# Layer 1's attention: products with the values in blocks of 32 tokens

## The chip, the cores and the metric

One core of one Trainium2 chip runs one program of four transformer-like layers. The metric is the device time of one execution in microseconds. All engines of the core take part: TensorE (PE in the rows, its weight loads PEld), VectorE (DVE), ScalarE (ACT), GpSimd (POOL), and SyncE (SP), which issues most DMAs.

## What is computed

The change touches only the attention of layer 1, a dilated attention without projections. Of 64 tokens of a segment, each head sees the 32 that have its parity, and within these it is a plain softmax attention with queries, keys and values all equal to the input:

```
w, r, H, hd = 64, 2, 16, 16            # segment, dilation, heads, head size
g = gather(xs, tokens 2*k + h % 2 of the segment)          # 32 tokens for each head
scores = einsum("bnhqd,bnhkd->bnhqk", g, g) * hd ** -0.5
out = einsum("bnhqk,bnhkd->bnhqd", softmax(scores), g)     # scattered back to the same tokens
x = x + out + moe(x_normalised)
```

The other half of layer 1 is a mixture of 32 experts, 4 per token. There are 4 x 512 = 2048 tokens of 256 channels. The normalised rows are sorted by expert: for each of a token's 4 choices its row is written to a slot in DRAM by an indirect DMA.

## The kernel before

The stage `slots_route` (line 2597) of layer 1 holds everything here. Tokens lie in 16 tiles of 128; tile n = 2g + p holds the tokens of parity p of a group g of 256, so a tile is four segments' worth of 32 tokens that attend to each other, and only the 8 heads of parity p have anything to do in it. The stage normalises x, computes the router's logits, picks 4 experts for each token and works out, on VectorE, the slot of each of the 4 x 16 x 128 rows. GpSimd then issues 64 scatters (`scatter`, line 2484, the instruction at L2487), each of one tile's 128 rows to one choice of expert; it begins as soon as the first choice's slots are known. VectorE goes on with the table of blocks and the weights of the experts (L2813 to L2841). Only then, in the program order of VectorE, comes `then.vector(dve)`, the attention.

`Attention1` (line 814) works tile by tile, with two buffers for everything (index p):

- ScalarE: `key_rows` copies the normalised rows, transposed, with the other parity's heads set to zero (L899); `weights` takes the exponential of the scores (L910); `copy_sums` copies the products with the values out of PSUM (L916); `value_rows` fills the values, 16 columns a head beside a column of ones, padded to 32 (L904).
- TensorE: `scores` multiplies 8 heads' keys by themselves, each a strip of 32 rows (16 of them zero) and 128 x 128 tokens (L859). `values` multiplies, for each of 8 heads, the values (128 tokens by 32 columns) by the exponentials (128 by 128 tokens), giving sums that are channel by token (L868). `back` turns them to token by channel, two transposes a tile (L876).
- VectorE: `mask` multiplies the exponentials (128 x 1024) by a 0/1 matrix that keeps the blocks of 32 tokens on the diagonal (L943). `finish` takes the reciprocal of the sums of the ones' column (L950), scales (L952) and adds to x (L957).
- The order is written out by hand in each engine's loop, by one tile ahead; semaphores count tiles. `mask`, `finish` alternate on VectorE; `scores`, `values`, `back` on TensorE.
- GpSimd: `wait_under_way` lets lot n of 8 scatters start only when 2(n - 2) + 1 masks are done, so that the attention's steps aren't held up behind them.

float32 matmuls show in the trace as two passes, each with a weight load, so 8 matmuls are 16 instructions.

The stage ends with a barrier of all engines. The next one, `slots_experts` (f_ in the names), loads the slots and begins its products. SyncE issues the loads of the biases (L2546, L2548) after VectorE has released its scratch, right ahead of the attention.

## Time and profile before

| | us |
|---|---|
| median of 3 runs (lowest, highest) | 2124.78 (2124.61, 2125.85) |
| the profiled execution | 2104.8 |
| its span, first to last instruction | 2102.9 |
| TensorE, VectorE, ScalarE, GpSimd busy | 1800.2, 1394.7, 740.2, 578.4 |
| mean granted TensorE clock | 0.925 |

The span is cut into stages by barriers. The one of this change lies at 130 to 261 us of the span, its attention at 170 to 226, its scatters at 164 to 256. An instruction's row in the timeline gives its start, its duration, and, in brackets, how long its engine was idle before it and who released it; "PEq L2651" and "POOLq L2651" are the barrier between two stages.

### The profile page before, as it was taken

The numbers are of one execution on the slowest core, as the hardware profiler recorded it, in microseconds if no ns is written. First come the engines' busy times: TensorE is split into PE (matmuls) and PEld (weight loads), VectorE is DVE, ScalarE is ACT, GpSimd is POOL, SyncE is SP. The second block draws the span as 40 slices with busy tenths as digits, with TensorE's granted clock in tenths as the row PEclk, the third lists the DMA queues.
The fourth block names the chain that finished last, engine by engine and source line by source line (L and its number), as shares of the span: only waits on it lengthen the run. The fifth ranks groups of instructions, "written<-read, shape, count | busy, mean of one in ns | idle before, by whom it ended". The sixth has DMA issues, their size and how long they took to land. (4 is left out here: it accounts for less than half of the span.)

```text
span 2102.9 us, 37015 instructions
## 1 busy us (share of the span) xinstructions
PE 1800.2 (86%) x13832; PEld 1433.3 (68%) x13832; DVE 1394.7 (66%) x2980; ACT 740.2 (35%) x1733; POOL 578.4 (28%) x550
## 2 busy tenths in 40 slices
PE   5844189944999999999999997999988997989995
PEld 2432177833899999999899985455566875767773
DVE  5588255548787777777787775666656777644444
ACT  2424134422333343434333333145534323322221
POOL 1326735540121221212221112622232103511111
PEclk9976699975999999999999997989998996999998
DMA  9448244443000000000000100000001007111114
GB/s 324 142 132 269 88 136 146 149 150 111 1 1 24 24 2 24 1 24 1 24 1 24 34 1 1 0 1 2 2 1 53 29 1 251 62 43 48 49 49 140
DMA packets 103060, 134.86 MB, mean 64 GB/s; under 512 B 11628, under 2 KB 78984, under 8 KB 102376
## 3 DMA queue, kind: packets, MB, share of 16 engines
q1 hardware_dynamic: 91800, 102.01, 15.5%
q0 software_dynamic: 11088, 30.49, 4.0%
q8 instruction: 116, 1.90, 0.4%
q14 instruction: 56, 0.46, 0.1%
HBM read 81.92 MB, written 50.54 MB: 63 GB/s over the span
## 5 line engine op out<-in xcount | busy, mean ns | idle before, releaser
L1138 POOL TENSOR_TENSOR a_rstd<-a_msq,consts 128x8 f32<-128x8 f32 x32 | 52.4, 1636 | 556.2 <-DVE a_msq L1493 556.2
L110 PE MATMUL a_ring<-a_w_hi,l_xnT_hi 128*128 128x256 f32 x512 | 152.0, 297 | 0.0
L110 PE MATMUL a_ring<-a_w_hi,l_xnT_lo 128*128 128x256 f32 x512 | 144.6, 282 | 0.0
L110 PE MATMUL a_ring<-a_w_lo,l_xnT_hi 128*128 128x256 f32 x512 | 144.4, 282 | 0.0
L2487 POOL DMA_INDIRECT l_slots_in<-xn,f_row_of x96 | 105.2, 1096 | 82.0 <-DVE f_row_of L2815 37.0
L3048 POOL DMA_INDIRECT l_pairs_out<-f_yb,f_to_row x96 | 94.6, 985 | 97.6 <-ACT f_yb L3023 70.9
L1450 DVE RECIPROCAL a_rT<-a_rT 128x256 f32<-128x256 f32 x64 | 111.5, 1744 | 0.0
L1739 PE MATMUL b_ring<-b_keys,b_qm 32*128 32x128 f32 (+2 forms) x896 | 94.2, 347 | 14.9 <-DVE b_nm L1952 9.4
L1905 ACT ACTIVATE b_work<-b_ring 128x1024 f32<-128x1024 f32 (+1 forms) x96 | 81.1, 881 | 65.1 <-PE b_ring L1746 64.1
L2942 PE MATMUL f_pgu<-f_gate_up_w,f_xT 128*128 x384 | 95.0, 391 | 5.5 <-ACT f_xT L3003 5.4
L1739 PEld LDWEIGHTS b_ring<-b_keys,b_qm 32*128 32x128 f32 x896 | 67.1, 198 | 46.4 <-issue 23.4
L110 PEld LDWEIGHTS a_ring<-a_w_hi,l_xnT_hi 128*128 128x128 f32 x512 | 97.5, 190 | 0.2 <-issue 0.2
L110 PEld LDWEIGHTS a_ring<-a_w_lo,l_xnT_hi 128*128 128x128 f32 x512 | 97.6, 191 | 0.0
L110 PEld LDWEIGHTS a_ring<-a_w_hi,l_xnT_lo 128*128 128x128 f32 x512 | 97.4, 190 | 0.0
L319 PE MATMUL n_turned<-consts,xn 128*128 128x128 f32 x96 | 24.9, 397 | 81.6 <-DVE xn L288 81.6
L3156 POOL DMA_INDIRECT l_pairs_out<-l_aT,f_to_row x39 | 37.2, 955 | 199.2 <-DVEq L3296 192.5
L3073 DVE TENSOR_TENSOR f_gu<-f_pgu,f_bias 128x256 f32<-128x256 f32 x96 | 40.8, 425 | 74.5 <-issue 41.4
L1746 PE MATMUL b_ring<-b_qm,b_keys 32*128 32x384 f32 (+3 forms) x512 | 87.4, 463 | 0.0
L1871 POOL TENSOR_SCALAR_AFFINE_SELECT b_work<-b_work 128x256 f32<-128x256 f32 x128 | 50.5, 407 | 127.3 <-ACT b_work L1905 125.3
L110 PE MATMUL a_ring<-l_xnT_hi,a_w_hi 128*128 128x512 f32 x192 | 79.8, 416 | 3.7 <-PEq L416 3.7
L2942 PEld LDWEIGHTS f_pgu<-f_gate_up_w,f_xT 128*128 128x128 f32 x384 | 70.7, 194 | 17.7 <-issue 9.3
L1407 ACT ACTIVATE a_on<-a_pde 128x128 f32<-128x128 f32 x256 | 66.7, 292 | 44.0 <-PE a_pde L1296 44.0
(514 smaller groups left out, 5359.6 us busy)
## 6 DMA issues: line engine op xcount, KB each, us to landing
l_slots_in<-l_zeros SPq DMA_DIRECT2D x4, 3120.0 KB, 22.2
f_xb<-l_slots_in SPq DMA_DIRECT2D x11, 1040.0 KB, 5.7
f_gate_up_w<-l_pairs_out SPq DMA_DIRECT2D x16, 512.0 KB, 8.7
l_slots_in<-l_zeros SPq DMA_DIRECT2D x3, 1690.0 KB, 19.0
f_xb<-l_slots_in SPq DMA_DIRECT2D x39, 130.0 KB, 2.1
f_down_w<-L_ffn_w_down_dram SPq DMA_DIRECT2D x1, 4096.0 KB
f_gate_w<-L_ffn_w_dram SPq DMA_DIRECT2D x2, 2048.0 KB, 11.1
f_up_w<-L_ffn_w_dram SPq DMA_DIRECT2D x2, 2048.0 KB, 19.7
```

The source lines that it names most:

```text
L110: ins = pe.matmul(out, a, b, start=start and k == 0, stop=stop and k == 2, **kw)
L1138: pool.tensor_tensor(rstd[:], msq[:], core.consts[:, C_HALF:C_HALF + 8], ALU.pow).then_inc(s["rstd_ready"], 1)
L1407: act.activation(sq[:, h, c, :], pov[:, h, c, :], ACT.Square, accum_out=ms[:, i:i + 1]).then_inc(s["sq_ready"], 1)
L1450: dve.reciprocal(rT[:, k % 2, cols], rT[:, k % 2, cols]).then_inc(s["r_ready"], 1)
L1739: return pe.matmul(ps[:, i, at:at + k1 - k0], qm[strip(j), p, c, b * T + q * P:b * T + (q + 1) * P], keys[strip(j), p, c, b * T + k0:b * T ...
L1746: return pe.matmul(ps[:, i, at:at + T - kb * P], keys[strip(j), p, c, b * T + kb * P:b * T + (kb + 1) * P], qm[strip(j), p, c, b * T + kb ...
L1871: ins = pool.affine_select(x, x, [[0, 2], [1, P]], ALU.is_ge, 0.0, 0, -1)
L1905: act.activation(probs[:, g % 2, 2 * pair:2 * pair + 2, T_AT[k]:T_AT[k] + w], slot["t", g, pair, k][:, :, 0:w], ACT.Exp).then_inc(s["exp_r ...
L2487: pool.indirect_dma_start(self.xs[:, :], bass.IndirectOffsetOnAxis(ap=self.row_of[:, k, t:t + 1], axis=0), core.rows[:, t, :], None).then_ ...
L2942: ins = pe.matmul(pgu[:, i % 2, j * 2 * I:(j + 1) * 2 * I], xT[:, i % 2, (j * DC + c) * P:(j * DC + c + 1) * P], r.gate_up[:, bass.ds(e, 1 ...
L3048: pool.indirect_dma_start(r.ys[:, :], bass.IndirectOffsetOnAxis(ap=r.to_row[:, b:b + 1], axis=0), yb[:, i % YR, j, :], None).then_inc(stor ...
L3073: dve.tensor_tensor(gu[:, i % GR, j].rearrange("p k i -> p (k i)"), pgu[:, i % 2, j * 2 * I:(j + 1) * 2 * I], r.bias[:, bass.ds(e, 1), :, ...
```

## The change

`values` no longer multiplies whole tiles. For each head and each block i of 32 tokens it multiplies the block's 32 x 32 exponentials, as the stationary side, by that block's values (32 tokens by 32 columns). Row strip i of TensorE's array and column strip i are used, and the result is token by channel, at the place where the finish wants it. Blocks off the diagonal are never read, so there is no mask; the result needs no turn, so there is neither the copy to SBUF nor `back`. `finish` waits for the products. The waits on `masked` (in `values` and in `wait_under_way`) become waits on `exp_ready`, with the same counts. The tile `sums` and four semaphores go.

```diff
         if n >= 2:
-            pool.wait_ge(self.masked, 2 * (n - 2) + 1)
+            pool.wait_ge(self.exp_ready, 2 * (n - 2) + 1)
...
         def values(g, p):
-            pe.wait_ge(self.masked, 2 * g + p + 1)
+            pe.wait_ge(self.exp_ready, 2 * g + p + 1)
             pe.wait_ge(self.vals_ready, 2 * g + p + 1)
-            pe.wait_ge(self.sums_copied, 2 * g + p + 1)
             pe.wait_ge(self.tile_done, 2 * g + p + 1)
             for h, (c, j) in enumerate(heads):
-                ins = pe.matmul(self.po[32 * j:32 * j + 32, p, 0, c, :], self.vals[:, p, h, :], self.e[:, p, h, :],
-                                start=True, stop=True)
+                for i in range(4):
+                    own = slice(32 * i, 32 * i + 32)
+                    ins = pe.matmul(self.po[own, p, 0, c, 32 * j:32 * j + 32], self.e[own, p, h, own],
+                                    self.vals[own, p, h, :], start=True, stop=True, skip_group_check=True)
             ins.then_inc(self.summed, 1)
 
-        def back(g, p):
-            pe.wait_ge(self.sums_copied, 2 * g + p + 3)
-            pe.wait_ge(self.tile_done, 2 * g + p + 1)
-            for c in range(DC):
-                ins = pe.transpose(self.po[:, p, 1, c, :], self.sums[:, p, c, :], self.core.ident)
-            ins.then_inc(self.out_ready, 1)
...
-        def copy_sums(g, p):
-            act.wait_ge(self.summed, 2 * g + p + 3)
-            act.wait_ge(self.out_ready, 2 * g + p + 1)
-            act.activation(self.sums[:, p], self.po[:, p, 0], ACT.Copy).then_inc(self.sums_copied, 1)
...
-        def mask(g, p):
-            dve.wait_ge(self.exp_ready, 2 * g + p + 1)
-            dve.tensor_tensor(self.e[:, p, :, :], self.e[:, p, :, :], core.blk.unsqueeze(1).to_broadcast([P, H2, P]),
-                              ALU.mult).then_inc(self.masked, 1)
-
         def finish(g, p):
             n = 2 * g + p
-            dve.wait_ge(self.out_ready, n + 3)
-            o = self.po[:, p, 1].rearrange("q c (j d) -> q (c j) d", d=self.PAD)
+            dve.wait_ge(self.summed, n + 3)
+            o = self.po[:, p, 0].rearrange("q c (j d) -> q (c j) d", d=self.PAD)
```

The calls of `mask`, `back` and `copy_sums` go from the loops; the order of what remains is the same.

## Rows read from the trace of the kernel before

**Rows 1.** Timeline (start us, us, engine, line): first, last scatter; the next stage.
```profile
164.41 1.17 POOL L2487 DMA_INDIRECT l_slots_in<-xn,f_row_of  x1 [23.40 <-DVE f_row_of L2815]
...
254.72 0.96 POOL L2487 DMA_INDIRECT l_slots_in<-xn,f_row_of  x1 [0.30 <-issue]
...
261.23 2.49 POOL L3042 MEMSET f_limits<- 128x128 f32 x2 [5.55 <-POOLq L2651]
261.24 1.28 ACT L2997 ACT_TABLE_LOAD   x1 [37.28 <-PEq L2651]
```

**Rows 2.** The timeline at the end of the attention.
```profile
224.23 0.29 DVE L952 TENSOR_TENSOR a_part<-a_out,a_inv 128x128 f32<-128x128 f32 x1
224.36 0.96 POOL L2487 DMA_INDIRECT l_slots_in<-xn,f_row_of  x1 [0.30 <-issue]
...
225.45 0.29 DVE L957 TENSOR_TENSOR x<-x,a_part 128x128 f32<-128x128 f32 x1
```

**Rows 3.** Groups (busy us, mean ns, idle) on GpSimd, 183.6-222.95, 223.05-255.75 us.
```profile
L2487 POOL DMA_INDIRECT l_slots_in<-xn,f_row_of x24 | 32.1, 1337 | 7.3 <-issue 7.0 <-DVE a_e L943 0.3
...
L2487 POOL DMA_INDIRECT l_slots_in<-xn,f_row_of x26 | 25.0, 960 | 7.9 <-issue 7.9
```

**Rows 4.** The timeline of VectorE and GpSimd, 218 to 221.1 us.
```profile
218.09 0.96 POOL L2487 DMA_INDIRECT l_slots_in<-xn,f_row_of  x1 [0.30 <-issue]
...
218.67 1.23 DVE L943 TENSOR_TENSOR a_e<-a_e,consts 128x1024 f32<-128x1024 f32 x1 [0.94 <-ACT a_e L910]
...
219.36 1.37 POOL L2487 DMA_INDIRECT l_slots_in<-xn,f_row_of  x1 [0.30 <-issue]
...
220.73 1.23 DVE L943 TENSOR_TENSOR a_e<-a_e,consts 128x1024 f32<-128x1024 f32 x1
...
221.03 1.76 POOL L2487 DMA_INDIRECT l_slots_in<-xn,f_row_of  x1 [0.30 <-issue]
```

**Rows 5.** Groups by line and shape, 165 to 260 us: mask, exponential, addition to x.
```profile
L943 DVE TENSOR_TENSOR a_e<-a_e,consts 128x1024 f32<-128x1024 f32 x16 | 19.5, 1225 | 9.4 <-ACT a_e L910 7.9 <-DVE x L957 1.0 <-DVE f_cw L2841 0.2
L910 ACT ACTIVATE a_e<-n_turned 128x1024 f32<-128x1024 f32 x16 | 16.4, 1024 | 3.6 <-PE n_turned L859 3.2
...
L957 DVE TENSOR_TENSOR x<-x,a_part 128x128 f32<-128x128 f32 x16 | 4.7, 292 | 0.5
```

**Rows 6.** The timeline of layer 1's expert stage: a scatter beside a VectorE step.
```profile
311.49 0.69 DVE L3081 TENSOR_TENSOR f_gu<-f_gu,f_limits 128x512 f32<-128x512 f32 x1
311.52 1.48 POOL L3048 DMA_INDIRECT l_pairs_out<-f_yb,f_to_row  x1 [2.10 <-ACT f_yb L3023]
```

**Rows 7.** The timeline of the routing stage: a scatter beside L2823.
```profile
174.59 0.96 POOL L2487 DMA_INDIRECT l_slots_in<-xn,f_row_of  x1 [0.30 <-issue]
174.60 1.25 DVE L2823 TENSOR_TENSOR f_bias<-p_upto,consts 128x1024 f32<-128x1024 f32 x1
```

**Rows 8.** The timeline of TensorE: scores and values of early and late tiles.
```profile
170.79 1.24 PE L859 MATMUL n_turned<-a_keys 32*128 32x128 f32 x16 [11.60 <-ACT a_keys L899]
...
184.07 1.08 PE L868 MATMUL a_out<-a_e,a_vals 128*32 128x128 f32 x16 [9.57 <-DVE a_e L943]
...
215.81 0.65 PE L868 MATMUL a_out<-a_e,a_vals 128*32 128x128 f32 x16 [1.27 <-DVE x L957]
...
216.75 0.73 PE L859 MATMUL n_turned<-a_keys 32*128 32x128 f32 x16
```

**Rows 9.** Stretches (bounds, us, busy us of each engine, clock, DMA share).
```profile
180.00:185.00 5.00, 0.93 (x16) 0.60 (x16) 4.66 (x6) 0.00 (x0) 3.94 (x4) 0.50 0.42 136
...
205.00:210.00 5.00, 3.34 (x68) 2.28 (x68) 3.85 (x9) 4.04 (x9) 4.08 (x4) 1.00 0.23 82
```

**Rows 10.** The timeline of TensorE in layer 2: passes with smaller blocks.
```profile
527.54 0.57 PE L1215 MATMUL a_pc<-a_e_tok,a_k_tok 128*64 128x64 f32 x12
...
533.00 0.87 PE L1252 MATMUL a_pc<-a_qT,a_hk 64*64 64x128 f32 x12
```

**Rows 11.** The timeline of VectorE at its first masks.
```profile
182.79 2.36 DVE L943 TENSOR_TENSOR a_e<-a_e,consts 128x1024 f32<-128x1024 f32 x2 [0.24 <-DVE f_cw L2841]
```

More of the change, by code:

```diff
@@ L823, in __init__ @@
         self.keys, self.e = st.sb("keys", [P, 2, DC, P]), st.sb("e", [P, 2, H2, P])
-        self.vals, self.sums = st.sb("vals", [P, 2, H2, PAD]), st.sb("sums", [P, 2, DC, P])
+        self.vals = st.sb("vals", [P, 2, H2, PAD])
         self.inv, self.part = st.sb("inv", [P, 2, H2]), st.sb("part", [P, 2, H2, HD])
@@ L827, in __init__ @@
         self.po = st.ps("out", [P, 2, 2, DC, P])
-        (self.ones, self.keys_ready, self.vals_ready, self.scores_ready, self.exp_ready, self.masked, self.summed,
-         self.sums_copied, self.out_ready, self.inv_ready, self.scaled, self.tile_done) = (st.sem(n) for n in (
-             "ones keys_ready vals_ready scores_ready exp_ready masked summed sums_copied out_ready inv_ready scaled "
+        (self.ones, self.keys_ready, self.vals_ready, self.scores_ready, self.exp_ready, self.summed,
+         self.inv_ready, self.scaled, self.tile_done) = (st.sem(n) for n in (
+             "ones keys_ready vals_ready scores_ready exp_ready summed inv_ready scaled "
              "tile_done").split())
@@ L886, in tensor @@
             values(g, 1)
-            back(g, 0)
             scores(g + 1, 1)
             values(g + 1, 0)
-            back(g, 1)
         values(GROUPS - 1, 1)
-        back(GROUPS - 1, 0)
-        back(GROUPS - 1, 1)
     def scalar(self, act):
@@ L911, in weights @@
                            scale=HD ** -0.5).then_inc(self.exp_ready, 1)
-        def copy_sums(g, p):
-            act.wait_ge(self.summed, 2 * g + p + 3)
-            act.wait_ge(self.out_ready, 2 * g + p + 1)
-            act.activation(self.sums[:, p], self.po[:, p, 0], ACT.Copy).then_inc(self.sums_copied, 1)
-        act.sem_inc(self.sums_copied, 2)
         key_rows(0, 0)
@@ L927, in scalar @@
             weights(g, 1)
-            copy_sums(g, 0)
             value_rows(g + 1, 0)
@@ L931, in scalar @@
             weights(g + 1, 0)
-            copy_sums(g, 1)
             value_rows(g + 1, 1)
         weights(GROUPS - 1, 1)
-        copy_sums(GROUPS - 1, 0)
-        copy_sums(GROUPS - 1, 1)
     def vector(self, dve):
         core, HD, H2 = self.core, self.HD, self.H2
-        def mask(g, p):
-            dve.wait_ge(self.exp_ready, 2 * g + p + 1)
-            dve.tensor_tensor(self.e[:, p, :, :], self.e[:, p, :, :], core.blk.unsqueeze(1).to_broadcast([P, H2, P]),
-                              ALU.mult).then_inc(self.masked, 1)
         def finish(g, p):
             n = 2 * g + p
-            dve.wait_ge(self.out_ready, n + 3)
-            o = self.po[:, p, 1].rearrange("q c (j d) -> q (c j) d", d=self.PAD)
+            dve.wait_ge(self.summed, n + 3)
+            o = self.po[:, p, 0].rearrange("q c (j d) -> q (c j) d", d=self.PAD)
             dve.reciprocal(self.inv[:, p, :], o[:, :, HD]).then_inc(self.inv_ready, 1)
@@ L960, in vector @@
         dve.sem_inc(self.tile_done, 2)
-        mask(0, 0)
-        mask(0, 1)
         for g in range(GROUPS - 1):
-            mask(g + 1, 0)
             finish(g, 0)
-            mask(g + 1, 1)
             finish(g, 1)
```

1 line of the change is left out of this document (removed).

## The prediction

> **What bounds the kernel now.** I read the timeline of the stage that holds the attention, from 160 to 262 us of the span. GpSimd issues its first scatter of layer 1's rows at 164.41 and the last of 64 at 254.72, ending at 255.68; nothing of the next stage starts before 261.23 [rows 1]. The same rows say who stood idle for that: ScalarE 37.28 us, GpSimd only 5.55. The attention's last VectorE step starts at 225.45 and takes 0.29 [rows 2]. So the attention is done 30 us before the scatters, and a faster attention by itself is worth nothing. What counts is what it does to the scatter queue.
>
> Then the scatters themselves. The last 26, with nothing beside them, take 0.960 us each; the 24 that run beside the attention take 1.337 [rows 3]. 24 x (1.337 - 0.960) = 9.05 us of stretch. The rows of one such stretch show its source [rows 4]: the scatter from 219.36 takes 1.37 and ends at 220.73, which is 0.83 after the mask (L943, 218.67 + 1.23 = 219.90) ends; the one from 221.03 takes 1.76 and ends at 222.79, 0.83 after the next mask's end (221.96). The one from 218.09 starts while VectorE is idle and takes 0.96 = 0.13 + 0.83, although a mask starts inside it. So 0.13 us into a scatter something is needed that a running mask holds, and the scatter waits for the mask's end. By this rule I went through all 24: 15 meet a mask, the remaining times of those masks give every excess within 0.02 us, their sum is 9.05, and no other instruction is needed to explain any of it.
>
> **The change, part by part.** (a) The mask goes: 16 VectorE instructions of 1.225 us [rows 5]. VectorE isn't the bound, so its 19.5 us buy nothing directly. The scatters lose their 9.05 us of stretch, and they are the path. What could take the mask's place is the only other step of the attention with both inputs in SBUF, the addition to x (L957, 0.29 us, 16 times [rows 5]). That kind holds scatters too: in the next stage a 0.69 us VectorE step on two SBUF inputs makes one take 1.48 [rows 6]. Steps that read PSUM (L950, L952) don't: the scatter at 224.36 starts inside a L952 and takes 0.96 [rows 2]. In the trace of before no scatter meets a L957, because the masks' ends set the beat. Bounds of this new cost: 0 and 16 x 0.29 = 4.6 us. With free beats, a scatter comes every 1.26 us (0.96 + 0.30 idle), so an addition is met with chance 0.29/1.26 = 0.23 and costs half its length: 16 x 0.23 x 0.145 = 0.5 us. I take 0.5, since the two beats (2.5 to 2.8 us a tile, 1.26 a scatter) have no reason to lock once the long instruction is gone, and keep 4.6 for the range.
>
> The Trainium skill ("SBUF — State Buffer", Who interferes with whom) says that a tensor_tensor with both inputs in SBUF contends with GpSimd's reads, but also that its probe saw no stall of a DMA's descriptor generation by it. By the second statement the mask costs the scatters nothing and this change is worth 0; the trace disagrees for these indirect scatters.
>
> One row of the trace does not fit the rule: a 1.25 us tensor_tensor (L2823) that begins 0.01 after a scatter does not stretch it [rows 7]. One of its inputs repeats a value along the row, so it may not use what the mask uses. That stays unexplained and is one reason for the "no change" case below.
>
> (b) TensorE's products. Before: 8 matmuls a tile, each shown as two passes, so 16 instructions with 128 columns, 0.65 us at clock 1.00 and 1.08 at 0.50 [rows 8, 9]. Now 32 matmuls = 64 instructions of 32 rows, 32 columns. No row shows this shape. From below: 12 passes of 64 columns (L1215) take 0.57 us [rows 10], and with some 0.27 for the last one, as for L868 in the same clock, the step is (0.57 - 0.27)/11 = 0.027 us; the 16 passes of L868 give (0.65 - 0.27)/15 = 0.025. From above: L1252, blocks of 64 rows and 64 columns that write different partitions of one bank, 12 in 0.87 [rows 10], gives (0.87 - 0.27)/11 = 0.055, with 128 columns to stream. I take 0.028 (its 32 columns are nearer to the first two): 63 x 0.028 + 0.27 = 2.0 us a tile; the bounds are 1.85 and 3.7. Added: some 1.4 us a tile. The weight loads double with the matmuls (64 for 16) and lie in the same steps, as they do in those rows.
>
> (c) The copy of the sums (16 ScalarE instructions) and the turn back (32 on TensorE) go: off the path, worth nothing alone. With them the chain values, copy, turn, finish shortens to values, finish.
>
> (d) The pace of a tile. Before it is 2.5 us: TensorE runs 68 instructions, two tiles of 34, in 5.00 us [rows 9]. After, TensorE: scores 0.73 + values 2.0 = 2.75 us; ScalarE was busy 4.04 in those 5 us, and the copies leave it; its exponential of 1.02 [rows 5] for the next tile lies beside the values. So the attention becomes bound by TensorE and a little slower a tile. It may compute tiles 0 and 1 before VectorE comes free at 182.8 [rows 11], then 14 tiles follow the first finish: 182.8 + 0.9 + 14 x 2.75 + 0.9 = 223, with before 225.7. At the upper bounds, 0.73 + 3.7 = 4.45: 247; with the clock at its lower level all along, 1.24 + 63 x 0.054 + 0.27 = 4.9: 253. The scatters end at 255.68 - 9.05 + 0.5 = 247.1. So I cost it at nothing: what hides it is the scatter queue, 24 us longer by the values taken. By the upper bounds that cover is just used up, and at the lower clock throughout 6 us of the gain would go; but the clock of before rises within the attention, from 0.50 to 1.00 [rows 9], and TensorE gets more work, not less.
>
> (e) GpSimd's waits. Each lot of 8 scatters from the third on waited for a mask (2(n-2)+1); now it waits for that tile's exponential, which comes earlier in the order. Before, the worst was 0.3 us, which is the usual gap between scatters. The last lot (scatter 56, near 237) needs 11 exponentials, there by about 210. Nothing. SyncE's loads of the biases stay behind the same semaphore, at 182.6, and nothing on SP's queue moves. VectorE's `finish` now waits for `summed`: only the next finish is queued behind it. TensorE's values now wait for no mask and no copy.
>
> (f) From the last scatter to the next stage lie 5.55 us (261.23 - 255.68) with all engines idle; I leave that as it is. Nothing later is tied to another clock than this stage's end, so the gain passes on whole.
>
> Sum: -9.05 + 0.5 = -8.5 us. The profiled execution took 2104.8 us (span 2102.9 and 1.9 around it); it would be 2096.3. The timed runs have a median of 2124.78, 20 us more, which the trace doesn't explain; I take the difference over as it is: 2124.8 - 8.5 = 2116.3 us.
>
> **The rivals.** *The additions take the masks' place* (the two beats lock): 4.6 us come back, the gain is 4.4, 2120.4 us. For it: before, the masks locked the beats in the same way [rows 4]. Against: 0.29 is short beside 1.26, and a hit moves the next scatter out of its way. (TensorE at the lower clock throughout, in (d), would end in the same place: 253, a gain of 2.5 us.)
>
> *No change*: the stretch is not the mask's, or the timed runs, 20 us apart from the profiled one, don't have it; or something else fills the scatters. 2124.8 us. For it: L2823 [rows 7]. Against: 15 of 15 stretches end 0.83 us after a mask, and 26 of 26 scatters without one take 0.960.
>
> *Slower*: the four row strips of a head write one bank, and each matmul must wait until the one before has left it. Then a pass costs its full 0.27 us: 64 x 0.27 = 17.3, with the scores 18.0 us a tile, from 173.1 (the first scores end at 170.79 + 1.24 [rows 8], then 1.02) 16 x 18.0 + 0.9: the attention ends at 462, 206 after the scatters of before, and the time is some 2331 us. It decides from the pace at which 14 tiles from 183.7 reach 255.7: (255.7 - 183.7 - 0.9)/14 = 5.1 us a tile, a step of (5.1 - 0.73 - 0.27)/63 = 0.065 us. Against: L1252 writes two row strips into one bank at 0.055 a step, not 0.27 [rows 10]. For: that is no faster than its 128 columns take alone, and near the 0.065. The Trainium skill ("TensorEngine Tiling (Array Packing)", Gotcha 1: PSUM Pressure) says that different row tiles cannot access the same PSUM bank at once; the strips here write disjoint partitions of one bank, and by that rule they would at least not run side by side. No row of 32 x 32 blocks exists here to decide it.
>
> **How the numbers follow.** Forecast 0.76, additions instead 0.12, no change 0.07, slower 0.05. Range 2113.5 to 2121.0: below, the full 9.05, 1.2 for the spread of the three runs and 1 for the 5.55 us gap; above, the 4.6 of the additions less the likely run spread. A measurement of this kernel can tell about 0.2% (4.2 us) from no change; of the second case half counts as within that, as does the third: faster 0.82, same 0.13, slower 0.05.
>
> **What would show it.** Right: scatters of 0.96 throughout except a few up to 1.25 that end 0.83 after a L957; the last starting near 246; the next stage near 252.7; 64 passes a tile in 1.8 to 2.2 us; attention done by 230. Wrong: stretched scatters with no VectorE step at their start, values of over 3.5 us a tile, or a GpSimd wait for the exponential.

## The result, and the profile after

The kernel before took 2125.38 us (median of 17 runs, 2120.38 to 2126.82), the changed kernel 2129.86 us (17 runs, 2127.65 to 2131.20): a ratio of 1.0022, with a 95% interval of 1.0015 to 1.0030. The forecast was 2116.3 (2113.5 to 2121.0). The change made the kernel slower by 4.5 us where 8.5 us of gain were expected. The profiled execution of the changed kernel took 2130.39 us, of which its span is 2128.5. In one of the later sets of runs a single slow run of the kernel before, of 6148.0 us, is left out of the comparison.

The stage in question first. The timeline of GpSimd in the changed kernel (start, duration, engine, line, then the idle time before it and what ended it), the lines that answer to [rows 1]:

```profile
201.05 0.96 POOL L2457 DMA_INDIRECT l_slots_in<-xn,f_row_of  x1 [6.23 <-ACT a_e L899]
...
215.55 0.96 POOL L2457 DMA_INDIRECT l_slots_in<-xn,f_row_of  x1 [4.68 <-ACT a_e L899]
...
229.23 0.96 POOL L2457 DMA_INDIRECT l_slots_in<-xn,f_row_of  x1 [3.84 <-ACT a_e L899]
...
243.74 1.02 POOL L2457 DMA_INDIRECT l_slots_in<-xn,f_row_of  x1 [4.68 <-ACT a_e L899]
...
257.30 0.96 POOL L2457 DMA_INDIRECT l_slots_in<-xn,f_row_of  x1 [3.68 <-ACT a_e L899]
...
266.16 0.96 POOL L2457 DMA_INDIRECT l_slots_in<-xn,f_row_of  x1 [0.30 <-issue]
...
281.06 2.49 POOL L3012 MEMSET f_limits<- 128x128 f32 x2 [13.93 <-POOLq L2621]
```

Beside the attention scatters take 0.96 us, as forecast; none is stretched to 1.4 or 1.8 as in [rows 4] (the one of 1.02 us begins while an addition to x runs that ends 0.18 us later). But GpSimd now stands 3.7 to 6.2 us before each of the last five lots of 8, "ACT a_e" being the exponential it waits for. The last scatter starts at 266.16, not near 246, and the next stage 13.9 us after its end, not 5.55: the attention itself now ends the stage. That stage starts at 281.06, where [rows 1] has 261.23.

The timeline of TensorE in the same kernel shows why the exponentials come late. L859 are the scores, L869 the products with the values, 64 passes a tile:

```profile
181.61 0.76 PE L869 MATMUL a_out<-a_vals,a_e 32*32 32x32 f32 x41 [8.37 <-issue]
...
191.12 0.27 PE L869 MATMUL a_out<-a_vals,a_e 32*32 32x32 f32 x2 [2.73 <-issue]
...
216.10 1.12 PE L869 MATMUL a_out<-a_vals,a_e 32*32 32x32 f32 x40
217.65 0.34 PE L869 MATMUL a_out<-a_vals,a_e 32*32 32x32 f32 x6 [0.42 <-issue]
...
272.35 1.08 PE L869 MATMUL a_out<-a_vals,a_e 32*32 32x32 f32 x64
273.65 1.24 PE L859 MATMUL n_turned<-a_keys 32*128 32x128 f32 x16 [0.22 <-ACT a_e L899]
274.81 1.08 PE L869 MATMUL a_out<-a_vals,a_e 32*32 32x32 f32 x64
```

Two paces stand side by side. After the scatters' end (267.1) a tile takes 2.46 us: scores 1.24, 64 passes 1.08 (272.35 to 274.81). While scatters are under way the same passes come one to six at a time, with gaps that end by "issue", which is to say by nothing that the profile shows. Three rows of the waits from 182 to 281 us (who waits <- for what: us in total, times, longest):

```profile
PE a_out L869 <- issue: 35.2, 47, 2.7
ACT a_vals L893 <- PE a_out L869: 33.0, 2, 23.7
POOL l_slots_in L2457 <- ACT a_e L899: 23.1, 5, 6.2
```

TensorE stood 35.2 us in 47 such gaps before its passes, ScalarE 33.0 in two waits for them, GpSimd 23.1 us for exponentials. The clock granted to TensorE was 0.50 in the stretches 165 to 182, 182 to 251 and 251 to 281 us; it did not rise as in [rows 9].

### The profile page after: what moved, and what is told of

The parts are those of the page before. It is cut to its first block and busy times, and to the rows that moved or that the text cites. A ratio compares the mean times of both kernels' runs of the same rounds, so it can differ in the third digit from the quotient of the medians.

```text
span 2128.5 us, 38405 instructions
## 1 busy us (share of the span) xinstructions
PE 1829.7 (86%) x14568; PEld 1456.1 (68%) x14568; DVE 1376.4 (65%) x2964; ACT 734.7 (35%) x1717; POOL 569.1 (27%) x550
## 5 line engine op out<-in xcount | busy, mean ns | idle before, releaser
L2457 POOL DMA_INDIRECT l_slots_in<-xn,f_row_of x96 | 94.5, 985 | 105.1 <-DVE f_row_of L2785 36.7
## 6 DMA issues: line engine op xcount, KB each, us to landing
f_gate_w<-L_ffn_w_dram SPq DMA_DIRECT2D x2, 2048.0 KB, 10.7
```

What stands on the lines that cost most here:

```text
L2457: pool.indirect_dma_start(self.xs[:, :], bass.IndirectOffsetOnAxis(ap=self.row_of[:, k, t:t + 1], axis=0), core.rows[:, t, :], None).then_ ...
```

## What the experiments were to tell, and two levels of time

The expectations name theories by letters; S: TensorE's instructions reach it too slowly while transfers run, and their number decides; B: the small passes in one bank stall by themselves; W: the waits of the lots are what costs; C: while scatters are under way all engines get instructions slowly, at one of two levels of time and not at the other. Others are explained where they stand. "Reach" is the theories' word: what a trace shows is that an engine takes up its next instruction late although its inputs are ready, not why.

The runs came in six sets, each on one chip and with the kernel before beside it. Its median was 2102.4 and 2104.0 us in the first two sets and 2125.2, 2124.7, 2122.1 and 2122.3 in the other four, with no mixture inside a set. I call these the lower and the upper level. The profile that stands before the prediction (2104.80) is of the lower level, the runs of the result are of the upper one. So each kernel is compared within its set. The first and the fourth set carry the same chip number (the machine isn't recorded), which speaks against the chip as the cause without excluding it; what sets the level stays open.

### At the lower level

**e1_before_look**: the kernel before, unchanged.

> The kernel before, unchanged, profiled once more. The profile on which the forecast rested took 2104.8 us while the timed runs of the same kernel have a median of 2125.4. If that profile was an unusual execution, this one takes 2120 to 2127 us and shows where the missing 20 us lie; the stage of the attention is the first place to look (next stage at 261 us if it is not there, at about 280 if it is). If the profile was usual and something outside the program makes the timed runs longer, this one shows the next stage near 261 us again.

2101.48 us; the next stage starts at 261.14. It is the profile of the first part again.

**e5_after**: the changed kernel, unchanged.

> The changed kernel itself, unaltered, timed where the kernel before may take about 2102 us rather than 2125. It asks whether its loss belongs to the program or to the chip. Theory W+S (GpSimd's lots wait for exponentials that TensorE's slow passes delay; the program alone makes it): the scatters stand in lots with idle time between them, the last scatter starts at about 266 us of the trace, the next stage at 281, and the time is 19 us over what the same kernel takes without the waits of the lots (2093.9), that is about 2113: a ratio of 1.005. Theory C (the slow trickle of TensorE's passes belongs to the slower chip): no passes in bursts of 0.72 us here, 2.46 us a tile throughout, the lots never wait long, the last scatter starts at 246 to 248 us, and the time is about 2094 us, a ratio of 0.996.

2092.28 us against 2104.02, ratio 0.9949 (0.9933 to 0.9966): here the change wins 10.7 us by the ratio, with an interval of 7 to 14, and 11.7 by the medians (four runs of it). **e6_before_look2** is the kernel before in that set:

> The kernel before, once more with a profile, so that each run of this set has a kernel before from the same chip. If the chip is one where it takes about 2102 us, the next stage starts at 261 us of the trace and the whole is 2101 to 2105. If it is one where it takes about 2125, the trace shows for the first time where those 20 us are: evenly over all stages (a slower clock of the chip: 1% more in each stage), or in a single stage.

2104.64 us. GpSimd's timeline, first, last scatter and next stage, of e6_before_look2 and then of e5_after:

```profile
164.18 1.17 POOL L2487 DMA_INDIRECT l_slots_in<-xn,f_row_of  x1 [23.28 <-DVE f_row_of L2815]
...
254.46 0.96 POOL L2487 DMA_INDIRECT l_slots_in<-xn,f_row_of  x1 [0.30 <-issue]
260.97 2.49 POOL L3042 MEMSET f_limits<- 128x128 f32 x2 [5.55 <-POOLq L2651]
```

```profile
163.38 1.17 POOL L2457 DMA_INDIRECT l_slots_in<-xn,f_row_of  x1 [23.23 <-DVE f_row_of L2785]
...
244.64 0.96 POOL L2457 DMA_INDIRECT l_slots_in<-xn,f_row_of  x1 [0.30 <-issue]
251.15 0.35 POOL L3012 MEMSET f_limits<- 128x128 f32 x2 [5.55 <-POOLq L2621]
```

From first to last scatter 90.28 us before and 81.26 after: 9.02 less, against the 9.05 of stretch in the forecast. The gap to the next stage is 5.55 in both. The forecast's mechanism is these 9.0 us; in this pair of profiles the changed kernel also begins its scatters 0.8 us earlier and gains 2.2 us behind the stage, which was not followed. TensorE in e5_after, beside scatters:

```profile
207.59 1.24 PE L859 MATMUL n_turned<-a_keys 32*128 32x128 f32 x16 [0.21 <-ACT a_e L899]
208.76 1.14 PE L869 MATMUL a_out<-a_vals,a_e 32*32 32x32 f32 x64
210.05 1.24 PE L859 MATMUL n_turned<-a_keys 32*128 32x128 f32 x16 [0.16 <-ACT a_e L899]
```

2.46 us a tile with scatters beside it, at a granted clock of 0.50. No trickle (passes that come a few at a time, with gaps between); only three longer gaps (0.53, 3.80 and 2.77 us, before 202). The longest wait of a lot is 0.3 us. So theory C stands here and W, S and B fall: the same program does not lose anything at this level.

**e2_after_no_lot_wait**: no waits of the lots.

```diff
-        if n >= 2:
-            pool.wait_ge(self.exp_ready, 2 * (n - 2) + 1)
+        pass
```

> The kernel after, without the waits of the scatter lots on the exponentials: GpSimd issues its 64 scatters without a stop. In the profile of after TensorE gets through its values slowly (17 us for the first tile, then 7 us a tile) exactly while scatters or loads are in flight, and at 2.45 us a tile when they pause. Theory S (TensorE's instructions reach it too slowly while other DMAs run): scatters end near 246, some 4 to 5 tiles are done by then, the other 11 follow at 2.45 us each: the next stage begins near 277, 3 to 5 us earlier than after (2125 to 2127). Theory W (the lots' waits are what costs): the next stage begins near 252, some 28 us earlier (about 2101).

2093.93 against 2102.44, ratio 0.9961 (0.9947 to 0.9975). First to last scatter 81.27 us, next stage at 252.42. At this level the waits cost nothing.

**e3_before_no_mask**: from the kernel before, the mask left out and what waited for it waiting for the exponential; the products then mix the four blocks of a tile.

```diff
-            pool.wait_ge(self.masked, 2 * (n - 2) + 1)
+            pool.wait_ge(self.exp_ready, 2 * (n - 2) + 1)
...
-        mask(0, 0)
-        mask(0, 1)
```

> The kernel before without the mask (the attention then mixes the four blocks of a tile; everything else is computed). It has the instruction count of before on TensorE. The forecast's main term alone: 15 stretches of scatters, 9.05 us, go, and nothing else changes. Theory S and the strips' theory B (the 32 x 32 blocks in one bank stall TensorE) both expect scatters of 0.96 us and no stalls of TensorE; 8 to 9.5 us faster than before if the scatters end the stage also in its usual executions.

2094.12, ratio 0.9961 (0.9947 to 0.9975); from first to last scatter 81.24 us. The mask alone carries the gain that was forecast: 8.3 us, by 9.0 us less of stretch (90.25 in e1_before_look).

The Trainium skill ("SBUF — State Buffer", Who interferes with whom) holds both that a tensor_tensor with two SBUF inputs contends with GpSimd's reads and that its probe saw no stall of descriptor generation by it; for these indirect scatters the second does not hold, since without the mask they take 9 us less.

**e4_before_quarters**: from the kernel before, each of the 8 products split into four of 128 rows and 32 columns, 64 passes; mask, copy and turn stay.

```diff
-                ins = pe.matmul(self.po[32 * j:32 * j + 32, p, 0, c, :], self.vals[:, p, h, :], self.e[:, p, h, :],
-                                start=True, stop=True)
+                for i in range(4):
+                    own = slice(32 * i, 32 * i + 32)
+                    ins = pe.matmul(self.po[32 * j:32 * j + 32, p, 0, c, own], self.vals[:, p, h, :],
+                                    self.e[:, p, h, own], start=True, stop=True, skip_group_check=True)
```

> The kernel before with each product with the values cut into four matmuls of 32 columns: 32 matmuls (64 passes) a tile as in after, but over all 128 rows and with no row strips; mask, copy and turn back stay. Theory S: TensorE stalls like in after, the attention is paced at 7 us a tile or more, the lots of scatters wait for it, and it is slower than before by 10 us or more. Theory B: no stalls, 1.6 us a tile for the values, the time of before within 2 us.

2101.19, ratio 0.9992 (0.9983 to 1.0002), no trickle, the next stage at 258.39. The attention ends at 239.28, 13.6 us later than in e1_before_look (225.67), and still 13.6 before the last scatter's end: at this level four times the matmuls cost nothing because the scatters cover them.

**e7_preset_zeros**: zeros set once, exponentials only on the diagonal blocks, 8 matmuls of 128 rows with the tile as weights.

```diff
+        pool.memset(self.e[:], 0.0).then_inc(self.ones, 1)
...
-                for i in range(4):
+                ins = pe.matmul(self.po[:, p, 0, c, 32 * j:32 * j + 32], self.e[:, p, h, :], self.vals[:, p, h, :],
...
+            for i in range(4):
+                own = slice(32 * i, 32 * i + 32)
+                ins = act.activation(self.e[own, p, :, own].rearrange("q (c j) k -> q j c k", c=DC),
```

> The same result by another road: the tile of exponentials is set to zero once, the exponentials are written by four ScalarE instructions to the four 32 by 32 blocks on the diagonal alone, and the products with the values are 8 matmuls of 128 rows with the whole tile as weights in place of 64 small ones; again no mask, no copy, no turn. The lots of scatters keep their waits. Theory S (the number of TensorE's instructions is what delays the exponentials): 16 instructions a tile arrive in time, the attention runs at the pace of the scores and of four exponentials (about 2.75 to 3.3 us a tile), the lots don't wait, the last scatter starts at about 246 us, the next stage at 252, and the time is 8.5 us under the kernel before, ratio 0.996. Theory W with another cause of the slow tiles (the TensorE clock, or its waits): the lots wait here as well, next stage at 270 us or later, ratio 1.00 or over.

2101.74, ratio 0.9994 (0.9982 to 1.0005). I missed the cost of its own products: 16 passes take 3.62 us where the small ones take 1.08, a tile 4.72 us, and the attention ended at 257.6, after the scatters:

```profile
202.42 3.62 PE L868 MATMUL a_out<-a_vals,a_e 128*128 128x32 f32 x16
205.97 1.24 PE L860 MATMUL n_turned<-a_keys 32*128 32x128 f32 x16
```

It tells nothing on S, only that the 32 x 32 form is the quicker of these two.

**e8_lots_held**: from the fifth lot on, lots wait for the last exponential.

```diff
-            pool.wait_ge(self.exp_ready, 2 * (n - 2) + 1)
+            pool.wait_ge(self.exp_ready, 16 if n >= 4 else 2 * (n - 2) + 1)
```

> The changed kernel, with the fifth and all later lots of scatters held until the last of the 16 exponentials. A look at the cause of the slow passes, not a better kernel. Theory S (TensorE's instructions reach it slowly while scatters are under way): as soon as the fourth lot's scatters have landed, every tile takes 2.45 us, with its 64 passes in 1.08, and the attention ends 20 us or more earlier than in the changed kernel (near 245 us); the 32 scatters that are left take 32 times 1.35 us after that. Rival B (the small passes in one bank stall by themselves) and rival K (the low granted clock): the slow tiles stay as slow without any scatter beside them, 7 us a tile, and the attention ends at about 280 us as it does there.

2119.55 us, next stage at 272.97. Tiles of 2.46 us before and in GpSimd's pause, so at this level it could not tell anything.

### At the upper level

**e9_before_look3**: the kernel before. **e10_after_again**: the changed one.

> The kernel before with a profile, for the chip of this set. It took 2125.4 us beside the changed kernel's 2129.9, and 2102 to 2104 on the chips of the two sets of experiments so far; its profile is from one of the latter kind. Theory C (on a slower chip TensorE's instructions come in a trickle while scatters are under way, which costs the kernel before something too): where it takes 2125, the products with the values or the scores show gaps put down to issue while the scatters run, and the next stage starts at 275 to 281 us of the trace in place of 261. Rival U (the slower chip is slower everywhere, by 1%): every stage is 1% longer and the next stage starts at 264. Where it takes 2102 to 2105 this look adds nothing.

> The changed kernel, unaltered, on the chip of this set. Theory C: on a chip where the kernel before takes 2102 to 2105 us, 2092 to 2094, ratio 0.995, with 2.46 us a tile; on one where it takes 2125, 2130, ratio 1.002, with the passes in bursts of 0.72 us. Rival P (it goes by the placement or the history of one run, not by the chip): the two kinds come mixed within one set, the same kernel at 2092 and at 2130.

2124.34 us for the kernel before (median of its set 2125.24); the changed kernel 2130.03, ratio 1.0021 (1.0011 to 1.0030), the result over again. Its ten runs lie between 2126.83 and 2132.78, none near 2092, so rival P falls. Of the 20 us between the levels, which the forecast had called unexplained, 17.6 arise in the very stage of the change: the next stage of the kernel before starts at 278.56 here and at 260.97 in e6_before_look2. The expert stage, where scatters also run beside other work, adds 5.2 (layer 2 begins its products at 535.03 for 512.26), and later stages give some 3 back. GpSimd, then TensorE, ScalarE and VectorE in that kernel:

```profile
227.34 0.96 POOL L2487 DMA_INDIRECT l_slots_in<-xn,f_row_of  x1 [4.86 <-DVE a_e L943]
...
253.48 0.96 POOL L2487 DMA_INDIRECT l_slots_in<-xn,f_row_of  x1 [4.72 <-DVE a_e L943]
...
263.13 0.96 POOL L2487 DMA_INDIRECT l_slots_in<-xn,f_row_of  x1 [0.30 <-issue]
278.56 0.34 POOL L3042 MEMSET f_limits<- 128x128 f32 x2 [14.47 <-POOLq L2651]
```

```profile
206.21 1.14 PE L859 MATMUL n_turned<-a_keys 32*128 32x128 f32 x16
...
208.57 0.45 PE L876 MATMUL a_out<-consts,a_sums 128*128 128x128 f32 x2
...
211.74 1.02 ACT L910 ACTIVATE a_e<-n_turned 128x1024 f32<-128x1024 f32 x1 [4.14 <-remote]
...
212.91 1.23 PE L859 MATMUL n_turned<-a_keys 32*128 32x128 f32 x16 [3.90 <-ACT a_e L910]
...
218.97 0.21 DVE L950 RECIPROCAL a_inv<-a_out 128x8 f32<-128x8 f32 x1 [4.88 <-remote]
...
219.98 1.08 PE L868 MATMUL a_out<-a_e,a_vals 128*32 128x128 f32 x16 [5.83 <-DVE x L957]
```

The scores end at 207.35 and ScalarE, idle, begins their exponential at 211.74; the turned sums are there at 209.02 and VectorE, idle, begins their reciprocal at 218.97. Here it is ScalarE and VectorE that take up their next instruction late, and TensorE's two long waits in these rows are for them. The attention, done 30 us ahead of the scatters in [rows 2], here ends at 278.06, 14 us after them. Rival U (1% everywhere) falls.

**e11_no_lot_wait_again**: the same edit as e2_after_no_lot_wait.

> The changed kernel without the waits of the scatters' lots, once more, on the chip of this set. On a chip where the kernel before takes 2102 to 2105: 2094, as before. On one where it takes 2125: theory W (there the waits of the lots are what costs, since GpSimd stands 45 us until the slow exponentials come): the scatters end at 247 us of the trace, the passes trickle until then, and after that each tile takes 2.46 us. By the trickle's pace in the changed kernel (about 7 us a tile beside scatters, from 184 us on) some 9 of 16 tiles are done by 247, the other 7 take 17 us, so that the next stage starts at about 266 and the time is 15 us under the changed kernel's: 2115, ratio 0.995 to the kernel before. Rival T (the tiles' own slowness is the bound, with or without the waits): next stage at 280, 2130.

2138.60, ratio 1.0067 (1.0050 to 1.0084): 8.6 us slower than with the waits. W falls here too, and my 2115 with it. TensorE, then GpSimd's last scatter:

```profile
239.39 0.37 PE L858 MATMUL n_turned<-a_keys 32*128 32x128 f32 x1 [2.43 <-issue]
242.19 0.37 PE L858 MATMUL n_turned<-a_keys 32*128 32x128 f32 x1 [2.43 <-issue]
...
259.19 1.24 PE L858 MATMUL n_turned<-a_keys 32*128 32x128 f32 x16 [0.22 <-ACT a_e L898]
260.36 1.08 PE L868 MATMUL a_out<-a_vals,a_e 32*32 32x32 f32 x64
```

```profile
245.26 0.96 POOL L2456 DMA_INDIRECT l_slots_in<-xn,f_row_of  x1 [0.31 <-issue]
...
290.45 2.49 POOL L3011 MEMSET f_limits<- 128x128 f32 x2 [44.23 <-POOLq L2620]
```

With scatters one behind the other, TensorE gets one matmul in 2.80 us for 38 us (214 to 252); its full pace comes back at 254.82, 8.6 us after the last scatter's end (246.22), with the usual 2.46 a tile. The lots' waits are no loss at this level: in their pauses the other engines work at full pace.

**e12_lots_held_again**: the same edit as e8_lots_held.

> The changed kernel, with the fifth and all later lots of scatters held until the last of the 16 exponentials, now timed. On a chip where the kernel before takes 2102 to 2105 us: 2119, the next stage at 273 us of the trace, as in its first look; it tells nothing new there. On one where it takes 2125: theory C (there the engines get their instructions slowly while scatters are under way, and only then): the tiles run at 2.46 us as soon as GpSimd pauses, near 197 us, the attention ends at about 230, the last scatter near 270, the next stage at 275 to 277, and the time is 2122 to 2125: 5 to 8 us under the changed kernel's 2130, though the same program is 27 us slower than it on the other chips. Rival D (something on that chip slows the small passes by themselves, scatters or not): tiles of 7 us in GpSimd's pause too, next stage at 300 or later.

2135.48, ratio 1.0050 (1.0033 to 1.0066). The time is 10 to 13 us over what I expected, and over the changed kernel's in place of under it, because the pause came with the fifth lot, at 212, not at 197; the scatters that were held then ended the stage (next at 289.46). The mechanism shows clearly. TensorE in GpSimd's pause (212.0 to 243.75) and at its end, with GpSimd's first scatter after it:

```profile
218.57 1.24 PE L859 MATMUL n_turned<-a_keys 32*128 32x128 f32 x16 [0.22 <-ACT a_e L899]
219.74 1.08 PE L869 MATMUL a_out<-a_vals,a_e 32*32 32x32 f32 x64
...
222.20 0.75 PE L869 MATMUL a_out<-a_vals,a_e 32*32 32x32 f32 x64
...
243.75 0.95 POOL L2457 DMA_INDIRECT l_slots_in<-xn,f_row_of  x1 [31.80 <-ACT a_e L899]
...
245.09 0.34 PE L869 MATMUL a_out<-a_vals,a_e 32*32 32x32 f32 x5 [0.41 <-issue]
```

Tiles of 2.46 us without scatters; 1.3 us after the first new one the trickle is back. Rival D falls. That the trickle comes with scatters under way and goes when they pause is shown; why it is absent at the lower level is not.

**e13_before_no_lot_wait**: the kernel before without its lots' waits (the mask's semaphore in place of the exponential's in the diff of e2).

> The kernel before without the waits of the scatters' lots. On a chip where it takes 2102 to 2105 with them: no change (its longest wait of that kind is 0.3 us). On one where it takes 2125: theory C says that the scatters then run without a pause until about 255 us, and the attention (68 TensorE instructions a tile in place of the changed kernel's 160) stands nearly still from 188 us on, as in the changed kernel without its waits, and needs 14 tiles of 2.5 us after the scatters' end: next stage at 285 to 290, 2131 to 2136, 6 to 11 us over the kernel before. Rival N (the number of instructions is all: 68 a tile get through beside scatters): next stage at 262 to 270, faster than the kernel before by 8 us or more.

2142.96, ratio 1.0083 (1.0067 to 1.0100), next stage at 299.85; worse than I expected by 7 to 12 us. N falls: with 68 instructions a tile the attention doesn't get through either. TensorE, ScalarE and VectorE:

```profile
184.13 1.24 PE L858 MATMUL n_turned<-a_keys 32*128 32x128 f32 x16
...
222.21 1.02 ACT L909 ACTIVATE a_e<-n_turned 128x1024 f32<-128x1024 f32 x1 [32.72 <-remote]
223.26 1.22 DVE L942 TENSOR_TENSOR a_e<-a_e,consts 128x1024 f32<-128x1024 f32 x1 [39.07 <-issue]
...
254.46 0.21 DVE L949 RECIPROCAL a_inv<-a_out 128x8 f32<-128x8 f32 x1 [29.97 <-remote]
```

ScalarE has its scores since 185.37, is free from 189.49 on, and begins the exponential at 222.21. VectorE's mask, in spite of "issue", waits for that exponential (it ends at 223.23), and so do TensorE's next scores (31.7 us). Then VectorE itself is late: its reciprocal stands right behind the mask (end 224.48), its input has been there since 191.72, and it begins at 254.46. So ScalarE and VectorE stand some 30 us each with their inputs ready, and TensorE waits for them.

**e14_no_mask_again**: the edit of e3_before_no_mask.

> The kernel before without its mask (each token's products then mix the values of the four blocks of its tile), once more. On a chip where the kernel before takes 2102 to 2105: 8 us less, ratio 0.996, as before. On one where it takes 2125: theory C: the end of the attention, not the scatter queue, sets the end of the stage there, so that the 9 us of stretch that go are worth little: what is saved is 1.2 us a tile in the fast stretches and one queue entry for the instructions, 0 to 6 us, ratio 0.997 to 1.000. Rival: the stretch counts there as well, 8 us, ratio 0.996.

2124.49 against 2124.69, ratio 0.9997 (0.9988 to 1.0007). At the upper level the mask's stretch is worth nothing: the same edit that gives 8.3 us at the lower one. The next stage starts at 278.49, as with the mask (278.56). If the parts add up, the changed kernel's loss, 2130.03 - 2125.24 = 4.8 us, lies in the other parts of the change, the small passes without copy and turn. The edit of e4_before_quarters, which has the many passes but keeps copy and turn, would have parted these two at this level; it was not run there.

**e15_preset_zeros_again**: the edit of e7_preset_zeros.

> The variant with zeros set once, exponentials written by four ScalarE instructions to the diagonal blocks, and 8 matmuls of 128 rows a tile (64 TensorE instructions a tile in all, scores included, in place of the changed kernel's 160). On a chip where the kernel before takes 2102 to 2105: no change against it, 2102, since its attention of 4.7 us a tile ends at 257. On one where it takes 2125: if the slow passes go by the number of instructions that TensorE needs while scatters run, it loses least of all: next stage at 262 to 270, 2108 to 2116, faster than both kernels. If any instruction that TensorE needs then comes late, whatever their number (theory C in its strong form, as in the kernel without waits, one instruction in 2.8 us): next stage at 285 or later.

2134.09, ratio 1.0048 (1.0031 to 1.0064), next stage at 285.99. The number of TensorE's instructions isn't all: with 64 a tile it is slower than the changed kernel with 160. Its tiles of 4.72 us and its four exponentials are slower by themselves, so it does not tell how much the number counts.

**e16_lots_of_4, e17_lots_of_4_sooner, e18_lots_of_4_earliest**: the changed kernel in lots of 4, with a wait for exponential n - 3 (from lot 4 on), n - 2 (from lot 5 on) or n - 1 (from lot 4 on). The edit of the second:

```diff
-    SENT = 8
+    SENT = 4
...
-        if n >= 2:
-            pool.wait_ge(self.exp_ready, 2 * (n - 2) + 1)
+        if n >= 5:
+            pool.wait_ge(self.exp_ready, n - 2)
```

> The changed kernel with its scatters in lots of 4 in place of 8; lot n waits for exponential n - 3, which keeps the old wait for every second lot and adds one between. Where the kernel before takes 2102 to 2105 us: the waits are met before they are asked for, 2092 to 2094, ratio 0.995, as the changed kernel. Where it takes 2125: theory C (while scatters are under way, instructions reach the engines slowly; in each pause of GpSimd they come at full speed, some 256 of TensorE's, after which the trickle begins again): the changed kernel needs 14.1 us for 8 scatters and two tiles (10.1 of scatters, 4 of pause). In lots of 4 a tile's 160 instructions fit into what one pause brings: 5.05 of scatters and 1 to 2 of pause, 6.0 to 7.0 us a tile, next stage at 272 to 281, 2120 to 2129, faster than the changed kernel by 1 to 10 us. Rival Q (a pause has to be some 4 us long before instructions come): 9 us a tile, next stage at 300 or later, 2145.

> The same in lots of 4, with lot n waiting for exponential n - 2 from the sixth lot on, so that GpSimd pauses from about 189 us of the trace on, where the passes trickled until 198 in the changed kernel. Where the kernel before takes 2102 to 2105: 2092 to 2096. Where it takes 2125: theory C: the first tile's values are done by about 192 in place of 198, and the attention ends with the last scatters instead of 4 tiles after them (10 us): next stage at 265 to 275, 2113 to 2122, faster than both kernels. Rival Q: as for the run before this, 2145.

> The changed kernel in lots of 4, lot n waiting for exponential n - 1 from the fifth lot on. Where the kernel before takes 2102 to 2105 us: TensorE does a tile in 2.46 and a lot takes 5.05, so the waits are met early: 2092 to 2096, ratio 0.995. Where it takes 2122 to 2125: theory C: GpSimd's first pause comes at 184.5 us of the trace in place of 191, so that the 24 passes left over of the first tile are through at 187 to 190 in place of 194; the cycle of 13.5 us for two tiles and 8 scatters stays, and the attention ends 4 to 6 us sooner than with the wait for exponential n - 2: next stage at 272 to 274, 2117 to 2120, ratio 0.997 to 0.999. Rival: an early pause only moves a later one (the scatters then end the stage): next stage at 277, no change, ratio 1.0005.

2125.47 (1.0017, 1.0008 to 1.0027) and 2123.61 (1.0005, 0.9995 to 1.0015) against 2122.09; 2124.85 (1.0011, 1.0002 to 1.0020) against 2122.26. Next stages at 281.74, 277.47 and 278.01. The second was expected at 2113 to 2122 and the third at 2117 to 2120: both miss. Pauses stayed 8 scatters apart; in e17_lots_of_4_sooner:

```profile
223.62 0.95 POOL L2457 DMA_INDIRECT l_slots_in<-xn,f_row_of  x1 [3.68 <-ACT a_e L899]
...
237.12 0.96 POOL L2457 DMA_INDIRECT l_slots_in<-xn,f_row_of  x1 [3.72 <-ACT a_e L899]
```

8 scatters and two tiles in 13.50 us, as with lots of 8 in the changed kernel (229.2 to 243.7 to 257.3: 14.5 and 13.6). What moved is the first pause, which ends at 203.26 in e16, at 196.21 in e17 and at 191.24 in e18. From e16 to e17 that gives back 4.3 us of the stage and 1.9 of the medians; the still earlier one gives nothing further, which is the rival's time; but its reason (the scatters would end the stage) is not what happened, since the attention still ends 8 us after the last scatter (277.50 for 269.51). None of the three beats the kernel before at this level, and they were not run at the lower one. A version better than both at both levels was not found; at the lower level none was measured clearly faster than the changed kernel.

## Why the prediction was wrong, by its own steps

**(a) The mask's stretch.** Right in mechanism and size at the level whose trace it was read from: 9.02 us by e5_after, 9.01 by e3_before_no_mask (81.24 against 90.25 in e1_before_look). The additions to x cost nothing measurable, under the 0.5 taken. Worth 0 at the upper level (e14_no_mask_again).

**(b) The passes.** Better than my lower bound. 64 take 1.08 us at a granted clock of 0.50 and 0.75 at 0.99 (the row at 222.20 of e12_lots_held_again), against 2.0 forecast and bounds of 1.85 to 3.7. (1.08 - 0.27)/63 = 0.013 us a pass. The forecast took 0.028 because a pass of 64 columns had cost 0.027; but at the same clock a pass of 128 columns costs (1.08 - 0.27)/15 = 0.054 [rows 8], four times 0.013, so against that row the step went with the columns, which the 64-column row had not shown. The rival of strips that each wait out 0.27 us is out by 20 times. The Trainium skill ("TensorEngine Tiling (Array Packing)", Gotcha 1: PSUM Pressure) says that row tiles cannot access one PSUM bank at the same time; the trace neither bears this out nor speaks against it: 0.013 us is what 32 columns would cost by that row if each pass streamed alone, so the four strips need not have run side by side, and they cost nothing on top of that.

**(c) Copy and turn.** Off the path at the lower level, as forecast. At the upper one they were not tested apart.

**(d) The pace and its cover.** 2.46 us a tile against 2.75 at the lower level, the attention ending at 227.5 with scatters until 245.6. One part was wrong in an instructive way: the clock did not rise, it was 0.50 all along (165 to 182, 182 to 251), and the forecast had reckoned 4.9 us a tile for that. The passes were so short that it did not matter; that the pace came out close to 2.75 is in part luck, with the scores at 1.24 for the 0.73 forecast and the passes at 1.08 for 2.0. At the upper level the step fails outright: 14 us for two tiles, and the attention is the end of the stage. The cover was 20 us thick in the trace and not there in the timed runs.

**(e) GpSimd's waits, "Nothing".** Right at the lower level (0.3 us), 23.1 us at the upper. But the cost isn't the wait itself: removing the waits makes it 8.6 us worse. They mirror exponentials that come late.

**(f) and the sum.** The gap of 5.55 holds in e5_after. The sum of the profiled execution, 2096.3, stands against 2092.6 measured; 1.5 of the 3.7 us are in the stage's end (251.15 for 252.7), of which 1.0 because the scatters began at 163.38 and not at 164.41; the others are behind it.

**The step that failed** is one sentence: "The timed runs have a median of 2124.78, 20 us more, which the trace doesn't explain; I take the difference over as it is." Of these 20 us, 17.6 arose in the attention's stage. In the timed runs the attention, not the scatter queue, ended that stage (278.06 against 264.09 in e9_before_look3), so a gain of the scatter queue was no gain. With it fell step (d), by which the attention was costed at nothing. My case "no change" had named this ("the timed runs, 20 us apart from the profiled one, don't have it") at a chance of 0.07; a difference twice as large as the forecast gain, and unlocated, deserved far more. The one case with the sign that came, "slower" at 0.05, had another mechanism (strips that wait in one bank) and 2331 us; none had the attention of the timed runs end its stage.

**The loss of 4.8 us**, from the traces: at the upper level the kernel before needs 26.1 us for 16 scatters and four tiles (227.34 to 253.48), 6.5 a tile; the changed one 13.6 to 14.5 for two, about 7.0 a tile. The next stage starts 2.5 us later (281.06 for 278.56), 3.9 in the pair of e10_after_again (282.46). The profiles differ by more than the medians do (2131.93 and 2124.34: 7.6 us for 4.8), and what lies behind this stage was not followed. That it is the number of small passes that makes the difference fits the bursts but is argued, not shown; against it stands e15_preset_zeros_again, with fewer instructions and slower, though its own tiles are longer too. So the cause of the 4.8 us stays open.

**Open:** by what way scatters hold the engines up, and what sets the level. That the instructions reach them late is the name of the theory, and the recorded instruction transfers don't bear it out: the pages of the changed kernel at the upper and at the lower level (e5_after) have

```profile
q8 instruction: 121, 1.98, 0.4%
```

```profile
q8 instruction: 122, 2.00, 0.4%
```

that is 121 and 122 transfers with the same share of the time. And from 185 to 257 us of e11_no_lot_wait_again, the stretch of the slowest trickle, the queues that moved anything are these two, with no instruction transfer among them:

```profile
q0 software_dynamic: 2402, 6.66, 26.4%
q1 hardware_dynamic: 680, 3.87, 16.7%
```

So TensorE was not waiting there for one of the recorded instruction transfers to end. Something between them and the engine, or a transfer that should have been asked for and wasn't, is not excluded.

## What to carry to other kernels

When the profiled execution and the timed runs differ by more than the gain at stake, find out first in which stage the difference lies; a gain read from one must not be carried to the other. A wait that paces an engine can be what lets the others work: take it away as an experiment before calling it cost or nothing. An off-path engine's added instructions are free only as long as it stays off the path: check that in the executions that are timed, too.

## What the runs showed of the hardware

- The same programs have two levels of time, 1% apart, that hold for a whole set of runs. At the upper one, while GpSimd's indirect scatters follow each other every 1.27 us, TensorE gets down to one matmul in 2.80 us (e11_no_lot_wait_again), and VectorE and ScalarE stand up to 30.0 and 32.7 us with their inputs ready (e13_before_no_lot_wait); the trickle begins again 1.3 us after a scatter starts (e12_lots_held_again; 2.1 us in the changed kernel, 217.65 after 215.55), and around a pause of GpSimd of 4.7 us (210.87 to 215.55) 134 passes go through at full pace (212.48 to 217.22 in the changed kernel: 14 + 64 + 16 + 40).
- 64 passes of 32 x 32 blocks, four row strips into one bank: 1.08 us at a granted clock of 0.50, 0.75 at 0.99, a quarter of the step of a 128-column pass; 16 passes with 128 x 128 weights and 32 columns take 3.62 at 0.50.
- A two-input VectorE step on SBUF stretches a scatter beside it: without the 16 masks 64 scatters take 81.2 us in place of 90.3, by two independent edits.
